# First attention of a six-block decoder: a projection behind every pair's values, the mixture's transposes and blocks placed in its last waits, and six weight units with buffers of their own

## The reference

```python
Q = jnp.einsum('bqd,hde->bqhe', x, W_Q) + b_Q        # K and V alike
scores = jnp.einsum('bqhe,bkhe->bhqk', Q, K) / np.sqrt(d_head)
scores = jnp.where(causal, jnp.float32(IGNORE), scores)
A = jax.nn.softmax(scores, axis=-1)
z = jnp.einsum('bhqk,bkhe->bqhe', A, V)
attn_out = jnp.einsum('bqhe,hed->bqd', z, W_O) + b_O
...
x = _layernorm(x + attn_out)
h = jax.nn.relu(jnp.einsum('edi,bsi->bsed', proj_in, x))    # the mixture
o = jnp.einsum('eid,bsed->bsei', proj_out, h)
...
x = _layernorm(x + gated sum of o over the experts)
```

## Time and profile before

| | |
|---|---|
| time of three runs | 1590.18 us median (1590.17 to 1592.86) |
| the profiled execution's own time | 1589.92 us |
| its span | 1588.1 us |
| PE busy | 1525.3 us, 96% |
| DVE, ACT, POOL busy | 993.2, 692.2, 203.5 us |
| the first attention | up to about 343 us of the span |

### The profile page before, as it was taken

The page is one execution under the profiler, slowest core; times in us unless marked ns, Lnnn a source line. Parts: engine busy times, 40 slices in busy tenths (PEclk is TensorE's granted clock), DMA queues, the critical chain, the costliest instruction groups (busy, mean ns, idle before and its releaser), DMA issues.

```text
span 1588.1 us, 28577 instructions
## 1 busy us (share of the span) xinstructions
PE 1525.3 (96%) x11028; PEld 1320.6 (83%) x11080; DVE 993.2 (63%) x2131; ACT 692.2 (44%) x1812; POOL 203.5 (13%) x215
## 2 busy tenths in 40 slices
PE   7999999889999999999999889999988999999997
PEld 6888888779999999988888767777766898999996
DVE  5877777865454544576666567788876465444547
ACT  3544444532222222223233267788875444444443
POOL 1322222220000000012000024122221300000001
PEclk9999999999999999999999999999999999999999
DMA  6000010000010110100000286688840000000101
GB/s 214 1 2 14 2 41 1 28 26 27 27 52 27 38 40 27 35 10 34 1 33 1 30 124 86 87 101 133 105 84 14 14 27 27 27 27 13 40 0 53
DMA packets 43081, 66.51 MB, mean 42 GB/s; under 512 B 4576, under 2 KB 33504, under 8 KB 42848
## 3 DMA queue, kind: packets, MB, share of 16 engines
q1 hardware_dynamic: 42976, 65.09, 20.3%
HBM read 36.24 MB, written 2.10 MB: 24 GB/s over the span
## 4 chain that ended last, share of the span: by engine, by line
PE 76%; issue 14%; DVE 6%; ACT 1%; DMA 1%; SPq 1%; POOL 0%; POOLq 0%; DVEq 0%; ACTq 0%
PE ps L85 19%; PE ps L86 19%; PE ps L87 18%; PE ps L1761 3%; PE ps L1775 2%; PE ps L1751 2%; PE ps L384 2%; PE ps L408 2%; PE ps L1806 2%; PE ps L395 1%; PE ps L1789 1%; DMA raw<-in_w_a 1%; PE ps L376 1%; DVE negm L534 1%; DVE wKT L523 1%
## 5 line engine op out<-in xcount | busy, mean ns | idle before, releaser
L831 ACT ACTIVATE m2hT_h<-ps 128x512 fp32r<-128x512 f32 x128 | 76.7, 599 | 278.5 <-PE ps L87 278.5
L955 DVE TENSOR_TENSOR m6hT_l<-m6h,m6hT_h 128x512 fp32r<-128x512 f32 x128 | 88.6, 692 | 168.9 <-ACT m6hT_h L829 168.9
L957 DVE SCALAR_TENSOR_TENSOR m2hT_l<-ps,m2hT_h 128x512 fp32r<-128x512 f32 x128 | 88.5, 691 | 163.5 <-ACT m2hT_h L831 163.5
L828 ACT ACTIVATE m6h<-ps,m6b 128x512 f32<-128x512 f32 x128 | 88.2, 689 | 197.7 <-PE ps L87 193.8
L1884 ACT ACTIVATE nPr<-ps,negm 128x128 f32<-128x128 f32 x512 | 147.1, 384 | 25.5 <-DVE negm L1981 25.1
L87 PE MATMUL ps<-w_h,m6hT_l 128*128 128x256 f32 x512 | 144.4, 282 | 0.0
L85 PE MATMUL ps<-w_h,m6hT_h 128*128 128x256 f32 x512 | 143.5, 280 | 0.6 <-DVE m6hT_l L955 0.6
L86 PE MATMUL ps<-w_l,m6hT_h 128*128 128x256 f32 x512 | 143.7, 281 | 0.0
L87 PE MATMUL ps<-m2w_h,m2hT_l 128*128 128x256 f32 x448 | 126.8, 283 | 0.0
L86 PE MATMUL ps<-m2w_l,m2hT_h 128*128 128x256 f32 x448 | 126.7, 283 | 0.0
L85 PE MATMUL ps<-m2w_h,m2hT_h 128*128 128x256 f32 x448 | 126.3, 282 | 0.0
(11 more groups left out here) (300 smaller groups left out, 4309.8 us busy)
## 6 DMA issues: line engine op xcount, KB each, us to landing
nKm<-nKc_h SPq DMA_DIRECT2D x64, 128.0 KB, 4.3
nQs<-nQc_h SPq DMA_DIRECT2D x64, 128.0 KB, 5.9
raw<-in_w_e1i SPq DMA_DIRECT2D x9, 512.0 KB, 3.3
raw<-in_w_e1o SPq DMA_DIRECT2D x9, 512.0 KB, 3.3
raw<-in_w_e6i SPq DMA_DIRECT2D x9, 512.0 KB, 3.3
raw<-in_w_e6o SPq DMA_DIRECT2D x9, 512.0 KB, 3.3
raw<-in_w_a SPq DMA_DIRECT2D x8, 512.0 KB, 4.6
nKm<-nKc_l SPq DMA_DIRECT2D x32, 128.0 KB, 4.9
```

Of the source, the lines that this page charges most:

```text
L828: nc.scalar.activation(c.h32[:, u % 2, :], ps[:, u % 2, :], ACT.Gelu, bias=bias)
L831: nc.scalar.activation(c.hT[0][:, ch, :], ps[:, u % 2, :], ACT.Relu).then_inc(c.s["hi_ready"], 1)
L955: last = nc.vector.tensor_tensor(c.hT[1][:, ch, :], c.h32[:, u % 2, :], c.hT[0][:, ch, :].bitcast(F32), ALU.subtract)
L957: last = nc.vector.scalar_tensor_tensor(c.hT[1][:, ch, :], ps[:, u % 2, :], 0.0, c.hT[0][:, ch, :].bitcast(F32), ALU.max, ALU.subtract)
```

## The change

It has three parts.

1. The table `w_of_step` puts one fill behind the values in each of a group's four steps (v2, q2, k1, v3), where there was one such fill in four steps (q1). The last step of a group has three fills (k2, k3, v3) where it had four k. In the last group v2 stands behind the values of its first step, and v3 in the second step.
2. In the steps behind step 28 PE does the mixture's x and blocks behind the second transposes, ahead of the output projection and the values, and x begins one step earlier (step 29). On DVE `z_lo` stands first in the steps from 29 on, ahead of the maxima. Two semaphore waits of the mixture's first transposes follow the fills v2 and v3.
3. Units 2 to 7 of the weights have raw buffers of their own, in memory that the second group's K and V take later. SP issues all eight units without a wait; bv, rows and the three later parts of x stand among and behind them. Unit 6 is split behind the second group's q0 in step 1 (before: behind its q2 in step 2), unit 7 behind q3 in step 2 as before.

The diff, whole:

```diff
--- before.py
+++ after.py
@@ -168,6 +168,7 @@
     consts_dve = sem("consts_dve")
     cols_loaded = sem("cols_loaded")
     small_loaded = sem("small_loaded")
+    bv_loaded = sem("bv_loaded")
     x_loaded = [sem(f"x_loaded{g}") for g in range(NG)]
     b2_loaded = sem("b2_loaded")
     zeroed = sem("zeroed")
@@ -236,6 +237,9 @@
     W.rec = m.place("wrec", [P, 3, 2 * QH], F32)
     W.bq8 = m.place("wbq8", [P, 8], F32)
     W.XT[1] = pair(m, "wXT1", [P, DC, WT])
+
+    a1_raw = raw + [Region(nc, m2_hidden_at + 4 * i * KB, 4 * KB).place(f"a1raw{i + 2}", [P, RAW], F32) for i in range(6)]
+    a1_loaded = raw_loaded + [sem(f"a1_loaded{i + 2}") for i in range(6)]
     W.s = signals("w", "g_full xt_hi g_evac bq_ready s_full s_max p_exp rec_done p_ready pt_full pt_ready z_full zt_hi zt_ready "
                        "o_full r_done xb_ready ln_var rstd_ready x_done gates_done")
     W.ctx_loaded = [sem("w_ctx_loaded0"), sem("w_ctx_loaded1")]
@@ -251,10 +255,12 @@
             return [[], [], [], []]
         own, later = [("v", (G, j)) for j in range(4)], G + 1 < NGW
         q, key = ([(kind, (G + 1, j)) for j in range(4)] if later else [] for kind in "qk")
-        return ([own[0:1], own[1:2], [("x", (G + 1, 0))] if later else [], []],
-                [own[2:3], own[3:4], q[0:1], q[1:2]],
-                [q[2:3], q[3:4], [], []],
-                [key[0:1], key[1:2], key[2:4], []])[k]
+        if not later:
+            return ([own[0:1], own[1:2], [], own[2:3]], [own[3:4], [], [], []], [[], [], [], []], [[], [], [], []])[k]
+        return ([own[0:1], own[1:2], [("x", (G + 1, 0))], own[2:3]],
+                [q[0:1], q[1:2], [], q[2:3]],
+                [q[3:4], key[0:1], [], key[1:2]],
+                [key[2:3], key[3:4], [], own[3:4]])[k]
 
     def w_start():
         return [("x", (0, 0))] + [(kind, (0, j)) for kind in "qk" for j in range(4)]
@@ -272,7 +278,7 @@
         return [(kind, (p - lag) // 2)] if (p - lag) % 2 == 0 and 0 <= (p - lag) // 2 < B else []
 
     A1_BY_ACT = (1, 2, 3, 4, 5)
-    W_X_AT, W_U_AT, W_W_AT = 30, NP, (28, 30)
+    W_X_AT, W_U_AT, W_W_AT = 29, NP, (28, 30)
 
     def w_following(p):
 
@@ -433,6 +439,11 @@
                     transpose_p(2 * (p - 2) + half)
                 for kind, i in f[half]:
                     fill(kind, i)
+            for kind, i in w_following(p):
+                if kind == "x":
+                    after["x"](i)
+                elif kind == "u":
+                    after["u"](0, i)
             for _, b in w_sequence("o", p, 4):
                 out_project(b)
             for kind, i in f[2]:
@@ -441,11 +452,6 @@
                 values(p - 2)
             for kind, i in f[3]:
                 fill(kind, i)
-            for kind, i in w_following(p):
-                if kind == "x":
-                    after["x"](i)
-                elif kind == "u":
-                    after["u"](0, i)
 
     def w_scalar(act, after):
         s = W.s
@@ -477,8 +483,8 @@
 
         x_hi(0)
         for k in A1_BY_ACT:
-            act.wait_ge(raw_loaded[k % 2], (U_A1 + (k - k % 2)) * 8 + 16)
-            nc.scalar.activation(wA1[0][:, k * RAW:(k + 1) * RAW], raw[k % 2][:, :], ACT.Identity).then_inc(split_act, 1)
+            act.wait_ge(a1_loaded[k], 16)
+            nc.scalar.activation(wA1[0][:, k * RAW:(k + 1) * RAW], a1_raw[k][:, :], ACT.Identity).then_inc(split_act, 1)
         for p in range(NP + 5):
             if 0 <= p - 3 < NP:
                 z_hi(p - 3)
@@ -524,6 +530,8 @@
                                                    col_bk1[:, 2 * j:2 * j + 2].unsqueeze(2).broadcast_to([P, 2, WT]), ALU.add)
                 else:
                     b, half = divmod(j, 2)
+                    if i == (0, 0):
+                        v.wait_ge(bv_loaded, 16)
                     last = nc.vector.tensor_tensor(W.V[G % 2][:, b, half * 8:(half + 1) * 8, :],
                                                    bank.rearrange("p (h e) -> p h e", h=8),
                                                    bv1[:, half * GT:(half + 1) * GT].rearrange("p (h e) -> p h e", h=8), ALU.add)
@@ -580,12 +588,14 @@
                 extra[kind, i]()
         for p in range(NP + 5):
             f = w_of_step(p)
+            if W_X_AT <= p < NP + 3:
+                z_lo(p - 3)
             if p < NP:
                 maximum(2 * p)
                 maximum(2 * p + 1)
             if 0 <= p - 1 < NP:
                 reciprocals(p - 1)
-            if 0 <= p - 3 < NP:
+            if 0 <= p - 3 < NP and p < W_X_AT:
                 z_lo(p - 3)
             for part in range(2):
                 for kind, i in f[part]:
@@ -722,8 +732,8 @@
             g, ch = divmod(k, DC)
             if ch == 0:
                 pe.wait_ge(*((N.s["x_done"], (NG + g + 1) * GB) if c.gelu else (W.s["x_done"], (g + 1) * GB)))
-            if k == 0 and not c.gelu:
-                pe.wait_ge(W.s["g_evac"], w_fill(NGW - 1, "v", 3) + 1)
+            if k < 2 and not c.gelu:
+                pe.wait_ge(W.s["g_evac"], w_fill(NGW - 1, "v", 2 + k) + 1)
             if c.gelu and k == 0:
                 pe.wait_ge(N.s["g_evac"], n_filled(NGG - 1, NF - 1))
                 pe.wait_ge(N.s["z_ready"], NSEQS - GB)
@@ -2043,20 +2053,24 @@
                 sp.dma_start(X[:, own, :], x_in[own].rearrange("b s d -> s b d")).then_inc(x_loaded[g], 16)
 
             def load_a1(k):
-                sp.dma_start(raw[k % 2][:, :], w_a1[:, k * RAW:(k + 1) * RAW]).then_inc(raw_loaded[k % 2], 16)
+                sp.dma_start(a1_raw[k][:, :], w_a1[:, k * RAW:(k + 1) * RAW]).then_inc(a1_loaded[k], 16)
 
             load_x(0)
             load_a1(0)
             sp.dma_start(cols[:, :], cols_in).then_inc(cols_loaded, 16)
-            load_a1(1)
+            for k in range(1, 6):
+                load_a1(k)
+            sp.dma_start(bv1[:, :], bv_in.partition_broadcast(P)).then_inc(bv_loaded, 16)
             sp.dma_start(rows[:, :], rows_in.partition_broadcast(P)).then_inc(small_loaded, 16)
-            sp.dma_start(bv1[:, :], bv_in.partition_broadcast(P)).then_inc(small_loaded, 16)
-            for k in range(2, 8):
-                sp.wait_ge(prep_done, k - 1)
-                load_a1(k)
-                if k >= 8 - (NG - 1):
-                    load_x(k - (8 - NG))
+            load_a1(6)
+            load_a1(7)
+            for g in range(1, NG):
+                load_x(g)
             w_sync(sp)
+
+            sp.wait_ge(prep_done, 8)
+            for j in range(2):
+                sp.sem_inc(raw_loaded[j], 3 * 16)
             load_unit(sp, U_E0, 0, w_e1i[0], RAW)
             load_unit(sp, U_E0, 1, w_e1o[0], RAW)
             mix_sync(sp, M2)
@@ -2105,7 +2119,7 @@
             nc.gpsimd.affine_select(out=band[:, :, :], in_=band[:, :, :], compare_op=ALU.is_ge, fill=NEG, base=8,
                                     pattern=[[0, QH], [1, S]], channel_multiplier=-1).then_inc(consts_pool, 1)
             pool.wait_ge(consts_dve, 7)
-            pool.wait_ge(small_loaded, 32)
+            pool.wait_ge(small_loaded, 16)
             w_pool(pool)
             pool.wait_ge(stage_done, 1)
             ffn_selector_pool(pool)
@@ -2163,7 +2177,11 @@
                     nc.vector.tensor_tensor(w[:, :, 1, :], col, w[:, :, 0, :].bitcast(F32), ALU.subtract).then_inc(consts_dve, 1)
 
             def split_a1(k):
-                split_unit(v, U_A1, k, cut(wA1, k * RAW, RAW), RAW)
+                w = cut(wA1, k * RAW, RAW)
+                v.wait_ge(a1_loaded[k], 16)
+                nc.vector.tensor_scalar(w[0], a1_raw[k][:, :], 1.0, None, ALU.mult).then_inc(split_hi, 1)
+                v.wait_ge(split_hi, k + 1)
+                nc.vector.tensor_tensor(w[1], a1_raw[k][:, :], w[0].bitcast(F32), ALU.subtract).then_inc(prep_done, 1)
 
             def high_a1():
 
@@ -2179,11 +2197,12 @@
                 v.wait_ge(split_act, A1_BY_ACT.index(k) + 1)
                 v.sem_inc(split_hi, 1)
                 w = cut(wA1, k * RAW, RAW)
-                nc.vector.tensor_tensor(w[1], raw[k % 2][:, :], w[0].bitcast(F32), ALU.subtract).then_inc(prep_done, 1)
-
-            def last_low():
-                low_a1(5)
-                v.wait_ge(small_loaded, 32)
+                nc.vector.tensor_tensor(w[1], a1_raw[k][:, :], w[0].bitcast(F32), ALU.subtract).then_inc(prep_done, 1)
+
+            def last_high(k):
+                split_a1(k)
+                if k == 7:
+                    v.wait_ge(small_loaded, 16)
 
             nc.vector.memset(mhalf[:, :], -0.5).then_inc(consts_dve, 1)
             v.wait_ge(consts_pool, 7)
@@ -2193,8 +2212,8 @@
             high_a1()
             w_vector(v, link, lambda: (low_first(), low_a1(1)),
                      {("q", (0, 0)): lambda: low_a1(2), ("q", (0, 2)): lambda: low_a1(3), ("q", (0, 3)): constants,
-                      ("k", (0, 1)): lambda: low_a1(4), ("k", (0, 2)): last_low,
-                      ("q", (1, 2)): lambda: split_a1(6), ("q", (1, 3)): lambda: split_a1(7)}, M2, m2)
```

(2 more changed lines are left out.)

## The result

| | before | after |
|---|---|---|
| median of the runs, us | 1590.18 (4 runs, 1589.54 to 1592.86) | 1580.63 (4 runs, 1579.65 to 1581.53) |
| the profiled execution's own time, us | 1589.92 | 1580.67 |
| its span, us | 1588.1 | 1578.8 |

The account below looks back on a forecast made before the run. PE, busy 96% of the span, was taken as the bound, so only its remaining waits and own length give time: 4.9 (middle groups) + 1.2 (start) + 2.9 (end) = 9.0, from 1590.18 to 1581.1 us, range 1578.5 to 1585.5.

Parts of the forecast that it names:

- Middle groups: Attention's middle groups: fills moved behind the values remove PE's wait for K's emptying, 0.84 us a group, 4.9 over six.
- The cover of 0.35 on DVE: A middle group's odd steps: DVE needs 7.6 of 7.97 us, so is through 0.35 before the next maximum could start.
- Start: Start and first group: earlier loads and moved fills shorten PE's waits, 0.7 and 0.6 less 0.1, gain 1.2 us.
- End: Attention's end, steps 29 to 31: waits 1.6, 0.5, 2.6, 0.4, sum 5.1 instead of 7.9; 2.9 gained with the starts.
- my lay-out has one fall, in the same place, at the price of before: Attention's end: granted clock falls once, some 3.3 us at half speed, costing 1.6; without it 1.6 less.
- Everything behind the attention is taken as it was: Behind the attention, from the mixture on: no change, since PE was without a wait when the mixture began.
- The sum: Whole kernel: 4.9 + 1.2 + 2.9 = 9.0 us gained, median 1581.1.
- The end gives nothing: Rival, steps 29 to 31: split ahead of maxima makes them wait for DVE, clock falls twice; 1584.0 us, chance 0.16.
- A new wait for K's: Rival, middle groups: odd steps lose 0.35 to 0.4 each on DVE, eating the 4.9; 1586.0 us, chance 0.08.
- slower by DVE's queue: Rival, odd steps: third fill's emptying delays the maxima, PE waits for values each time; 1593.5 us, chance 0.04.
- Crowded loads: Rival, start: x and unit 0 land later, PE starts up to 1.24 later; 1582.3 to 1583.6 us, chance 0.05.
- The waits are only moved: Rival, all three terms: exponentials set the pace, not fills, so each about a quarter; 1588 us, chance 0.05.

Follow-up runs that it names:

- fills_only: Kernel before with part 1 alone, the new table of fills (unit 6 split behind the second group's q0): 1587.09 us, ratio 0.9977.
- the repetition: The changed kernel run again unaltered for a second profile ("again" in the table): 1579.97 us, ratio 0.9931 against the kernel before.
- end_only: Kernel before with part 2 alone (mixture's x and blocks ahead of output projection and values, x from step 29, z_lo first): 1583.33 us, ratio 0.9950.
- splits_early: The change with both splits of the mixture's first weights in step 28 on DVE, ahead of v2's emptying: 1574.8 us, ratio 0.9895.
- loads_only: Kernel before with part 3 alone (own raw buffers, loads issued without waits; unit 6 split as before): 1589.0 us, ratio 0.9988.
- last_group_old: The change with the last group's fills where they were before (v0, v1 in step 28; v2, v3 in step 29): 1575.15 us, ratio 0.9904.
- z_behind: The change with z's low part behind the maxima and reciprocals from step 29 on, as before: 1578.61 us, ratio 0.9918.

## Why the prediction was right

**Middle groups: right, in size too.** 4.94 over six groups, 0.82 each, against 4.9 and 0.84. fills_only has the 38.30 without the other parts. The price that was taken over from a q fill is right for a v fill too: 1.52 against 1.53. The idle time of 0.16 ahead of L376 is gone, but it stood there only where the first mask's record is missing. The cover of 0.35 on DVE was 0.42, so no wait took the place of K's.

**Start: too small, for a part that isn't the change's.** 2.5 at step 4 against 1.2; the repetition stood 1.4 ahead there. PE's slow cadence at the start (0.21 us a matmul of 256 columns; 0.12 later) ended at 11.81 after and at 14.42 before. The rows give the granted clock as 1.00 all through it, so they don't say what makes it. When it ends differs between executions of one kernel, so the kernels can be compared at either:

| slow cadence ends | old loads, first scores | new loads, first scores |
|---|---|---|
| 14.3 to 14.6 | 25.18 (before), 24.6 (end_only) | 24.14 (again), 24.27 (splits_early) |
| 11.6 to 11.8 | 25.17 (fills_only) | 23.05 (after), 23.11 (loads_only) |

The loads are worth 0.3 to 1.0 where the slow cadence ends late, about the 0.7 of the prediction, and 2.1 where it ends early. The other five profiles with the new loads lie between, in the same order (12.0 to 14.2 for the cadence, 23.16 to 24.13 for the scores). With the old loads an early end is worth nothing: fills_only waits for the emptying of q1, behind unit 2, what PE had won.

```profile
15.92 0.39 PE L85 MATMUL ps<-wXT_h,wA_h 128*128 128x256 f32 x1 [1.44 <-DVE wQT L521]
```

**End: the waits right to 0.1, the clock wrong.** Predicted 1.6, 0.5, 2.6 and 0.4; measured 1.54, 0.23, 2.52 and 0.50, and 0.30 ahead of the masks of step 30 that the lay-out didn't have. The sum is the same 5.1, and the place of each as described, the split within 0.6 us of v2's emptying. The step that failed is "my lay-out has one fall, in the same place, at the price of before": in this execution there was none, and the end gave 4.4 instead of 2.9. In the repetition there was one of 3.4 us, some 11 us earlier in the program, and the end was only 0.2 longer (50.07 against 49.90): PE, slowed from 300.9 to 304.3, came 1.1 later to step 31 and then waited 1.7 instead of 2.5 for the second transposed half. So of the 1.7 that such a fall costs by itself, the waits behind it paid most.

The Trainium skill (TensorE: Matmul & The Clock Gate, "HAM oscillation — how this bites in real kernels") makes such a fall the price of every long enough gap. Its own example has longer gaps than the waits at the attention's end, so these don't test it at that length, and the prediction leaned on it too much. At the lengths that stand here it gives no forecast: ahead of the values of step 31 the clock went to half behind a gap of 2.52 in end_only and stayed at 1.00 behind gaps of 2.52 (after) and 2.53 (last_group_old); behind the 1.54 of step 29 it stayed in the first profile and fell in the repetition.

**Behind the attention: wrong.** "Everything behind the attention is taken as it was" missed 2.6 of give-back. 1.6 to 1.7 is the longer half-clock stretch at 691 to 698. Of the other 1.0 the change has lost 0.6 by about 950 us and the rest by 1300 (it is ahead by 9.7 and 9.3 there), and nothing behind that; what made it isn't shown. The repetition of the same program gave back 0.4.

**The sum** of 9.0 against 9.3 is therefore better than its terms: +1.3 at the start and +1.5 at the end, less 2.6 behind it. The first and the last hang on the execution and not on the change (0.2 and 0.4 in the repetition). The one at the end is there in both, since the fall was missing in one and paid by the waits in the other. Between after and its repetition the medians agree to 0.7, and both ratios are near 0.993, so some 10 us are solid; that the forecast hit the median by 0.5 is luck.

**The rivals.** "The end gives nothing" is false with 4.4 and 4.3, though its mechanism, a split ahead of the maxima, is real: two kernels that take it away in different ways have an end that is 2.2 to 2.4 shorter (last_group_old in step 29 only). "A new wait for K's" and "slower by DVE's queue" are false: no wait of PE stands in the rows from 80 to 275 us, and DVE has 0.42 of slack. "Crowded loads" is false for PE: it starts at 8.47 as before (8.50). But the crowding is there, at unit 1, whose high part ACT began at 7.73 before and now

```profile
8.87 1.06 ACT L487 ACTIVATE wA_h<-raw 128x1024 fp32r<-128x1024 f32 x1 [2.37 <-DMA raw<-in_w_a]
10.13 1.06 ACT L487 ACTIVATE wA_h<-a1raw 128x1024 fp32r<-128x1024 f32 x1 [0.21 <-DMA a1raw<-in_w_a]
```

while unit 2 follows at 10.13 (before 12.93) and unit 5 at 13.91 (before 22.10). "The waits are only moved" is false in the middle groups and partly true of z's low part (z_behind).

## What to carry to other kernels

When a piece of work moves to a later place on the engine that produces it, look at what is queued behind its consumer on the other engine: here v2's emptying held back a weight split that needed nobody, through 3.16 idle us, and then let it run in front of the maxima. Put work that depends on nothing ahead of the instruction that waits, in the gap that the wait opens; here that was worth 2.2 to 2.4 us, half of what the end gave. The worth of a change of filling depends on what stands beside it, so parts have to be tried alone and together: the fills alone lost 2.8 at the end, x ahead of the values alone gained 5.3, and together they gave 4.4 and not the sum.

## What the hardware showed beside this

- The granted clock decides a few us between executions of one program. The kernel before took 1587.4 to 1592.6 us in 17 runs, with a mean granted clock of 0.992 in the fastest and 0.989 in the slowest. Profiled executions at 0.992 and 0.993 had 17.0 us at half clock up to PE's last instruction, those at 0.989 and 0.990 had 27.2 or 30.6. Below a difference of some 3 us one profile against another proves nothing; lengths between landmarks in stretches at full clock (a group: 38.30 in eight kernels, 39.12 in three) repeat to 0.01.
- Stretches at half clock came in lengths of 3.4, 6.8 and 10.2 us, behind the attention at the same few places of the program, and which length a place got changed between executions.
- Records of matmuls can be missing from a trace in a regular way (33 or 34 masks of 64 in all traces but one), which moves a landmark by 0.23 us and can stand in the rows as idle time that ended by "issue".
- SP's DMA issues can take long: one of x takes 0.45 us alone, and the three later parts took 8.01 us behind the eight units; the first issue of ctx came at 15.31. A full queue would do that, but no row shows the queue. Nobody waited for either here.

```profile
7.26 8.01 SPq L2053 DMA_DIRECT2D X<-in_x  x3
15.31 2.28 SPq L298 DMA_DIRECT2D ctxg<-in_ctxT  x1
```
